# Feed-forward: first mark of a block by a scan and 32x32 transposes on VectorE, its blocks sent to their partitions by DMAs

## The chip, the core and the metric

The kernel runs on one core of a Trainium2 chip: TensorE (PE), VectorE (DVE), ScalarE (ACT), GpSimd (POOL) and SyncE (SP, which here only issues DMAs), with SBUF and PSUM beside them and 16 DMA engines. The metric is the time of one execution in device microseconds; the kernel before takes 1007.56 us (median of 3 runs, 1005.65 to 1009.1).

## What is computed

x is (4, 512, 512): 2048 tokens of width 512. One attention layer (32 heads of 16, 8 key heads) with residual and layer norm, then a sparse feed-forward with residual and layer norm:

```
inter = xf @ c1_w.T @ c2_w.T            # rank 16, 1792 columns
blk   = inter.reshape(tokens, 56, 32)
idx   = argmax(blk, -1) + arange(0, 1792, 32)
h     = relu(sum_m w1[idx] * xf)        # one of 32 rows of w1 in each block
out   = sum_k h * w2t[idx]
x     = layernorm(x + out)
```

`argmax` takes the first of equal maxima, and a token keeps one column of each block of 32.

## The kernel before, in words

The first 593 us (`_attend`) are projections and attention; the change touches only constants there. The feed-forward (`_feed_forward`) works densely: for all 1792 columns it computes h, and sets to zero what was not chosen. It goes over 4 batches b of 512 tokens, and in each over 14 tiles m of 128 columns. One (b, m) is called a slot here, "slot 1,3" is b = 1, m = 3.

In a slot, in TensorE's program order: `inner_up` of this slot (twelve 512-column matmuls into ps_h, three per 128 rows of the contraction, since every operand is split into a high and a low part), `first_marks` (one matmul into ps_z), `inner_down` of the slot before (twelve matmuls into ps_out), and `turn_mask` of the next slot (four bf16 transposes into ps_t). Up to two preparing steps (`slot_steps`) stand between the halves of inner_up and of inner_down.

Preparing steps: a mark step multiplies u (rank 16) by 448 columns of c2 (a chunk; four chunks c to a batch, four token tiles t to a chunk); VectorE reduces each block of 32 to its maximum and compares, which leaves a mask of ones at the maxima, tokens on partitions. In the pick, columns must be on partitions: TensorE turns the mask, ScalarE copies it, and the matmul with `first` (1 on the diagonal, -2 for earlier columns of the same block) gives exactly 1 at the first one. `pick` on VectorE keeps relu(h) where ps_z is 1; ScalarE and GpSimd split the result into g_h and g_l, which ps_out of the next slot reads. Other steps turn tiles of x (xf_sb, xt_h, xt_l), form u ("U"), and in slots 0,4 to 0,7 multiply by wo for the last batch's attention output.

Marks of chunks 1 to 3 of a batch are made in its slots 0-1, 2-5 and 6-7 (6-8 in batch 0), those of chunk 0 in the last slots of the batch before. For b > 0 VectorE also adds ps_out to the residual in slot 0 (`add`), takes statistics in slot 1 and normalises in slot 2.

SP's queue is one program in order. At the start of this half: denominators, w2 tiles 0 and 1, four attention loads, the reciprocals (`inverted`, L936), their spread copy (L938), then by slot the w2 loads (L908), x loads (L902), y loads and stores. A wait on SP holds everything behind it. ScalarE takes w2 tile m+1 before relu of slot m in batch 0 (`high_w2`).

## Time and profile before

| | |
|---|---|
| median of 3 runs | 1007.56 us |
| profiled execution | 998.58 us, span 996.8 us |
| granted TensorE clock, mean | 0.944 |
| busy: PE, DVE, ACT, POOL | 91%, 56%, 44%, 19% |
| L1222 ps_z matmuls in the last 337 us | 49, 390 ns each |
| L1199 ps_t transposes there | 192, 222 ns each |
| L1090 pick there | 49, 691 ns each |

The profile is one execution seen by the hardware profiler. Busy time counts an engine's instructions; matmuls overlap in the pipeline, so their spans add up to more than the time between their starts. "Idle before" is the time in which the engine had nothing running, with what released it. An engine's busy share alone says little: what counts is which wait ends last.

### The profile page before, as it was taken

To read this page: it belongs to the slowest core of one execution; us is meant where nothing else is said; L and a number is where in the kernel's file an instruction comes from. 1 tells how busy PE (TensorE), PEld (TensorE's weight loads), DVE (VectorE), ACT (ScalarE), POOL (GpSimd) and SP (SyncE) were. 2 spreads that over 40 slices of the span, in tenths; PEclk is the share of its full clock that TensorE was granted. 3 is DMA by queue.
4 is the path that set the end of the run, shared out by engine and by line. 5 is a ranking of instruction groups with operands and counts; after the bars stand their busy time and mean duration, and the time that the engine had idled before them with its cause. 6 is when DMAs were issued, how large, how long until landed. Compare 5 with 4: busy or idle time off the path is not lost. (4 is left out here: it accounts for less than half of the span.)

```text
span 996.8 us, 12134 instructions
## 1 busy us (share of the span) xinstructions
PE 908.2 (91%) x4472; PEld 533.0 (53%) x4472; DVE 562.4 (56%) x743; ACT 442.9 (44%) x821; POOL 193.1 (19%) x183
## 2 busy tenths in 40 slices
PE   5868999999899998999989975999999999999995
PEld 3745543333334333343333434777777777777774
DVE  4636567888656885468866533545563365326413
ACT  3302466777654775456765542322222222222231
POOL 6302003730210002100021002333321222122221
PEclk8889999999989998599988978999999999999998
DMA  8466535643342243323433124214030002001101
GB/s 249 160 205 240 169 110 159 175 123 91 91 117 69 76 134 80 97 85 79 135 82 109 34 97 102 82 44 155 14 116 11 1 3 103 2 1 43 42 1 42
DMA packets 50858, 92.99 MB, mean 93 GB/s; under 512 B 5648, under 2 KB 13840, under 8 KB 50288
## 3 DMA queue, kind: packets, MB, share of 16 engines
q1 hardware_dynamic: 49312, 87.05, 29.3%
q0 software_dynamic: 1488, 5.16, 1.9%
q8 instruction: 36, 0.59, 0.2%
q14 instruction: 22, 0.18, 0.1%
HBM read 56.80 MB, written 34.87 MB: 92 GB/s over the span
## 5 line engine op out<-in xcount | busy, mean ns | idle before, releaser
L509 DVE TENSOR_REDUCE neg_max<-ps_max 128x2 f32<-128x1024 f32 x256 | 302.9, 1217 | 90.1 <-PE ps_max L670 89.7
L486 ACT ACTIVATE probs<-ps_st 128x512 f32<-128x512 f32 x496 | 270.2, 595 | 142.6 <-PE ps_st L707 139.7
L707 PE MATMUL ps_st<-q,k 50*128 50x512 f32 x496 | 181.9, 511 | 28.5 <-ACT probs L486 27.6
L707 PEld LDWEIGHTS ps_st<-q,k 50*128 50x128 f32 x496 | 71.9, 192 | 203.1 <-ACT probs L486 156.8
L670 PE MATMUL ps_max<-k,q 48*128 48x512 f32 x512 | 152.8, 452 | 14.0 <-DVE neg_max L509 9.2
L721 PE MATMUL ps_pv<-probs,v 128*32 128x512 f32 x1024 | 147.3, 649 | 5.9 <-ACT probs L486 2.3
L978 POOL TENSOR_TENSOR g_l<-picked,g_h 128x512 fp32r<-128x512 f32 x56 | 73.1, 1306 | 286.9 <-ACT g_h L1017 286.9
L1003 ACT ACTIVATE mask_t<-ps_t 128x512 bf16<-128x512 bf16 x56 | 33.4, 597 | 163.6 <-PE ps_t L1199 163.6
L1211 PE MATMUL ps_h<-xt_h,w_h 128*128 128x512 f32 x224 | 93.8, 419 | 8.0 <-ACT relu L1010 8.0
L1073 DVE TENSOR_REDUCE top<-ps_prep 128x14 f32<-128x448 f32 x62 | 38.6, 623 | 99.0 <-PE ps_prep L1188 98.8
L670 PEld LDWEIGHTS ps_max<-k,q 48*128 48x128 f32 x512 | 75.6, 199 | 28.9 <-DVE neg_max L509 13.5
L1090 DVE SCALAR_TENSOR_TENSOR picked<-ps_z,relu 128x512 f32<-128x512 f32 x56 | 38.7, 691 | 90.6 <-ACT relu L1010 90.6
L1211 PE MATMUL ps_h<-xt_h,w_l 128*128 128x512 f32 x224 | 88.8, 397 | 0.0
L1211 PE MATMUL ps_h<-xt_l,w_h 128*128 128x512 f32 x224 | 88.8, 397 | 0.0
L1010 ACT ACTIVATE relu<-ps_h 128x512 f32<-128x512 f32 x56 | 33.6, 599 | 102.2 <-PE ps_h L1211 102.2
L1234 PE MATMUL ps_out<-w_h,g_h 128*128 128x512 f32 x160 | 71.2, 445 | 0.0
L1234 PE MATMUL ps_out<-w_h,g_l 128*128 128x512 f32 x160 | 63.2, 395 | 0.0
L1234 PE MATMUL ps_out<-w_l,g_h 128*128 128x512 f32 x160 | 63.0, 394 | 0.0
L1211 PEld LDWEIGHTS ps_h<-xt_h,w_h 128*128 128x128 f32 x224 | 43.1, 192 | 15.5 <-ACT relu L1010 8.1
L412 POOL TENSOR_TENSOR att<-att,inv 128x512 f32<-128x512 f32 x12 | 14.8, 1270 | 172.4 <-DMA inv<-reciprocals 172.4
L1211 PEld LDWEIGHTS ps_h<-xt_h,w_l 128*128 128x128 f32 x224 | 42.7, 191 | 9.4
L1211 PEld LDWEIGHTS ps_h<-xt_l,w_h 128*128 128x128 f32 x224 | 43.2, 193 | 6.2
(159 smaller groups left out, 1141.2 us busy)
## 6 DMA issues: line engine op xcount, KB each, us to landing
q_stacks<-parts SPq DMA_DIRECT2D x48, 256.0 KB
q<-q_stacks SPq DMA_DIRECT2D x64, 192.0 KB, 3.6
sums<-stage SPq DMA_DIRECT2D x32, 256.0 KB, 3.4
k<-k_stacks SPq DMA_DIRECT2D x64, 96.0 KB, 3.1
x_raw<-xT SPq DMA_DIRECT2D x16, 256.0 KB, 8.5
yf<-after_attention SPq DMA_DIRECT2D x4, 1024.0 KB, 5.3
w_raw<-w POOLq DMA_DIRECT2D x16, 224.0 KB, 3.1
w_raw<-w SPq DMA_DIRECT2D x14, 256.0 KB, 2.9
```

Source lines behind the costliest of these rows:

```text
L486: nc.scalar.activation(probs[kt % 2][:, r], score_bank(n, r), ACT.Exp, scale=float(HD) ** -0.5).then_inc(exp_done, 1)
L509: nc.vector.tensor_reduce(neg_max[n % 2][:, i // 2, :, i % 2], ps_max[i % 2][:], AX.X, ALU.max, negate=True).then_inc(max_red, 1)
L670: mm = nc.tensor.matmul(ps_max[i % 2][:, a], q[n % QR][64 * a:64 * a + STACK, j, t * P:(t + 1) * P], k_[n % QR][64 * a:64 * a + STACK, :], ...
L707: nc.tensor.matmul(score_bank(n, r), k_[n % QR][64 * a:64 * a + ROWS, kt * P:(kt + 1) * P], q[n % QR][64 * a:64 * a + ROWS, j, :], start=T ...
L721: last = nc.tensor.matmul(ps_pv[32 * r:32 * r + VW], v[f % 2][:, kt, g], probs[kt % 2][:, r], start=(kt == 0), stop=(kt == TT - 1))
L978: nc.gpsimd.tensor_tensor(g_l[m % 2][:], picked[m % 2][:], g_h[m % 2][:].bitcast(F32), ALU.subtract).then_inc(g_ready, 1)
L1003: nc.scalar.activation(mask_t[m % 2][:], ps_t[:], ACT.Copy).then_inc(mask_t_ready, 1)
L1010: nc.scalar.activation(act_r[m % 2][:], ps_h[:], ACT.Relu).then_inc(relu_ready, 1)
L1073: nc.vector.tensor_reduce(top[t % 2][:], src, AX.X, ALU.max).then_inc(prep_half, 1)
L1090: nc.vector.scalar_tensor_tensor(picked[m % 2][:], ps_z[:], 1.0, act_r[m % 2][:], ALU.is_equal, ALU.mult).then_inc(picked_ready, 1)
L1211: last = nc.tensor.matmul(ps_h[:], w[:, k, m * P:(m + 1) * P], xx[b % 2][:, k], start=(k == 0 and n == 0), stop=(k == KT - 1 and n == 2))
L1234: last = nc.tensor.matmul(ps_out[t][:], g[m % 2][:, t * P:(t + 1) * P], w2_tile(*w, m), start=(m == 0 and n == 0), stop=(m == MT - 1 and n ...
```

## The change

The mask turn, its copy and the first-mark matmul go. After the comparison VectorE runs a scan over the 448 columns, rank = rank * doubling + equal, where `doubling` is 2 everywhere and 0 at the start of each block: from the first mark on the value is 1 and is then doubled, so exactly the first marked column has the value 1. VectorE then transposes each 32x32 square, and SP sends the squares to their partitions: 16 DMAs a chunk, each 32 partitions by 3 or 4 blocks by 128 bf16 values. For that u is written with its tokens in another order. The pick compares rank_t in SBUF instead of ps_z. ps_h and ps_prep get two banks each. Relu writes where the pick writes. The w2 tiles are loaded to where their low part will be; the waits for the memory under them move from ScalarE to SP.

```diff
+            def spread_ranks(b, c):
+                i = b * NC + c
+                first, last = c * CH // BLK, (c + 1) * CH // BLK
+                sp.wait_ge(rank_turned, TT * (i + 1))
+                if b:
+                    sp.wait_ge(picked_ready, (b - 1) * MT + (last - 1) // 4 + 1)
+                for o in range(4):
+                    blocks = [n for n in range(first, last) if n % 4 == o]
+                    m = slice(blocks[0] // 4, blocks[-1] // 4 + 1)
+                    for g in range(4):
+                        src = turned[i % 2][BLK * g:BLK * (g + 1), blocks[0] - first:blocks[-1] - first + 1:4]
+                        sp.dma_start(rank_t[BLK * o:BLK * (o + 1), m, P * g:P * (g + 1)],
+                                     src.rearrange("p n t k -> p n (t k)")).then_inc(rank_in[i % 2], DMA)
...
+            spread_ranks(0, 0)
 
             at = (NB - 1) * NH * S
             sp.wait_ge(inverted, 1)
...
+                    if m in (1, 5, 7 if b else 8):
+                        spread_ranks(b, (1, 5, 7 if b else 8).index(m) + 1)
+                    if b + 1 < NB and m == (12 if b else 13):
+                        spread_ranks(b + 1, 0)
...
-                act.wait_ge(mask_turned, i + 1)
-                nc.scalar.activation(mask_t[m % 2][:], ps_t[:], ACT.Copy).then_inc(mask_t_ready, 1)
...
-                nc.scalar.activation(act_r[m % 2][:], ps_h[:], ACT.Relu).then_inc(relu_ready, 1)
+                    act.wait_ge(g_ready, i - 1)
+                nc.scalar.activation(picked[m % 2][:], ps_h[i % 2][:], ACT.Relu).then_inc(relu_ready, 1)
...
-                nc.vector.tensor_copy(u[:], bank[0:80]).then_inc(prep_half, 1)
+                nc.vector.tensor_copy(_by_group(u[:]), _in_order(bank[0:80])).then_inc(prep_half, 1)
...
+                    dve.wait_ge(prep_done, n + 1)
+                    nc.vector.tensor_tensor_scan(rank[:], doubling[:], equal[:], 0.0, ALU.mult, ALU.add
+                                                 ).then_inc(rank_done, 1)
+                    dve.wait_ge(rank_done, TT * i + t + 1)
+                    if i >= 2 and t == 0:
+                        dve.wait_ge(rank_in[i % 2], 16 * DMA * (i // 2))
+                    nc.vector.transpose(turned[i % 2][:, :, t], rank[:].rearrange("p (n k) -> p n k", k=BLK)
+                                        ).then_inc(rank_turned, 1)
...
-                dve.wait_ge(z_done, i + 1)
+                dve.wait_ge(rank_in[c % 2], 16 * DMA * (c // 2 + 1))
                 dve.wait_ge(relu_ready, i + 1)
-                nc.vector.scalar_tensor_tensor(picked[m % 2][:], ps_z[:], 1.0, act_r[m % 2][:], ALU.is_equal,
+                nc.vector.scalar_tensor_tensor(picked[m % 2][:], rank_t[:, m], 1.0, picked[m % 2][:], ALU.is_equal,
                                                ALU.mult).then_inc(picked_ready, 1)
...
-                    last = nc.tensor.transpose(ps_t[:, t * P:(t + 1) * P], mask[:, t, m * P:(m + 1) * P], ident16[:])
-                nc.tensor.matmul(ps_z[:], first[:], mask_t[m % 2][:], start=True, stop=True).then_inc(z_done, 1)
```

SP's order at the start of the feed-forward, before (den_last are the denominators, w_h<-sums the attention loads into memory of w2's high part, w_l<-reciprocals the spread copy, w_raw<-w a w2 tile):

```order
L926 DMA den_last<-sums 128x1x128
L908 DMA w_raw<-w 128x512 x2
L931 DMA w_h<-sums 128x1x512 x4
L936 DMA reciprocals<-inv_den_last 128x128 [waits invertedf]
L938 DMA w_l<-reciprocals 128x1x2048 [waits rdenf_out]
L908 DMA w_raw<-w 128x512 [waits w2_low] x3
L918 DMA yf<-x 128x4x512 [waits attf_split]
```

and now:

```order
L951 DMA w_h<-sums 128x1x512 x4
L918 DMA rank_t<-turned 32x4x128 [waits rank_turned]
L918 DMA rank_t<-turned 32x4x128 x7
L918 DMA rank_t<-turned 32x3x128 x8
L957 DMA reciprocals<-inv_den_last 128x128 [waits invertedf]
L959 DMA w_l<-reciprocals 128x1x2048 [waits rdenf_out]
L928 DMA w_raw<-w 128x512 [waits w2_low] x2
L918 DMA rank_t<-turned 32x3x128 [waits rank_turned]
L918 DMA rank_t<-turned 32x3x128 x7
L918 DMA rank_t<-turned 32x4x128 x8
L928 DMA w_raw<-w 128x512 [waits w2_low]
L938 DMA yf<-x 128x4x512 [waits attf_split]
```

Chunk 0's sixteen DMAs stand between the attention loads and the reciprocals, chunk 1's between w2 tiles 3 and 4.

SP's order in slots 0,8 to 0,10 now (xf_sb are the x loads; chunk 3's DMAs stand ahead of the third of them):

```order
L903 DMA xf_sb<-after_attention 128x512
L928 DMA w_late<-w 128x512 [waits prep_mm,w2_low]
L918 DMA rank_t<-turned 32x3x128 [waits rank_turned]
L918 DMA rank_t<-turned 32x3x128 x7
L918 DMA rank_t<-turned 32x4x128 x8
L903 DMA xf_sb<-after_attention 128x512 [waits prep_mm]
L928 DMA w_late<-w 128x512 [waits w2_low]
L903 DMA xf_sb<-after_attention 128x512 [waits prep_mm]
```

Before, the same x load had only a w2 load ahead of it.

VectorE's order in slot 1,0 before (a mark step, the pick, a mark step, the four adds):

```order
L1073 TENSOR_REDUCE top<-ps_prep 128x14 [waits prep_mm]
L1078 TENSOR_TENSOR mask<-ps_prep,top 128x448 [waits mask_turned,prep_half]
L1090 SCALAR_TENSOR_TENSOR picked<-ps_z,relu 128x512 [waits g_ready,relu_ready,z_done]
L1073 TENSOR_REDUCE top<-ps_prep 128x14 [waits prep_mm]
L1078 TENSOR_TENSOR mask<-ps_prep,top 128x448 [waits prep_half]
L1097 TENSOR_TENSOR yf<-ps_out,yf 128x512 [waits out_mm,yf_in]
L1097 TENSOR_TENSOR yf<-ps_out,yf 128x512 x3
```

and now:

```order
L1093 TENSOR_REDUCE top<-ps_prep 128x14 [waits prep_mm]
L1095 TENSOR_TENSOR equal<-ps_prep,top 128x448 [waits prep_half]
L1103 SCALAR_TENSOR_TENSOR rank<-doubling,equal 128x448 [waits prep_done]
L1108 STREAM_TRANSPOSE turned<-rank 128x14x32 [waits rank_in1,rank_done]
L1116 SCALAR_TENSOR_TENSOR picked<-rank_t,picked 128x512 [waits relu_ready,rank_in0]
L1093 TENSOR_REDUCE top<-ps_prep 128x14 [waits prep_mm]
L1095 TENSOR_TENSOR equal<-ps_prep,top 128x448 [waits prep_half]
L1103 SCALAR_TENSOR_TENSOR rank<-doubling,equal 128x448 [waits prep_done]
L1108 STREAM_TRANSPOSE turned<-rank 128x14x32 [waits rank_done]
L1123 TENSOR_TENSOR yf<-ps_out,yf 128x512 [waits out_mm,yf_in]
L1123 TENSOR_TENSOR yf<-ps_out,yf 128x512 x3
```

Each mark step is four instructions long instead of two, and the pick can wait for the DMAs of its chunk (rank_in).

## Rows read from the trace of the kernel before

**Rows 1.** Windows: us, then busy time of PE, PEld, DVE, ACT, POOL, PEclk, DMA, GB/s

```profile
896.00:912.00 16.00, 16.00 (x77) 12.39 (x76) 12.39 (x25) 4.60 (x9) 4.63 (x4) 1.00 0.00 1
614.00:615.00 1.00, 0.00 (x0) 0.00 (x0) 0.00 (x0) 0.00 (x0) 0.00 (x0) 0.78 0.29 57
```

**Rows 2.** Chain that ended last: start us, us, engine, tile, line

```profile
716.65 1.44 PE ps_h L1211 x6
...
723.12 1.44 PE ps_h L1211 x6
...
946.64 2.80 PE ps_h L1211 x12
949.67 2.79 PE ps_out L1234 x12
952.70 2.80 PE ps_h L1211 x12
```

**Rows 3.** Timeline of VectorE, start of the feed-forward: start us, us, instruction

```profile
593.71 0.62 DVE L1073 TENSOR_REDUCE top<-ps_prep 128x14 f32<-128x448 f32 x1 [10.15 <-PE ps_prep L1188]
594.37 0.62 DVE L1078 TENSOR_TENSOR mask<-ps_prep,top 128x448 bf16<-128x448 f32 x1
594.91 0.61 DVE L1073 TENSOR_REDUCE top<-ps_z 128x14 f32<-128x448 f32 x1
...
596.10 0.94 DVE L1122 RECIPROCAL inv_den_last<-den_last 128x128 f32<-128x128 f32 x1
```

**Rows 4.** Timeline of SP's issues, start of the feed-forward

```profile
597.24 0.48 SPq L936 DMA_DIRECT2D reciprocals<-inv_den_last  x1
603.32 0.59 SPq L938 DMA_DIRECT2D w_l<-reciprocals  x1
603.95 17.89 SPq L908 DMA_DIRECT2D w_raw<-w  x3
633.22 0.38 SPq L918 DMA_DIRECT2D yf<-x  x1
```

**Rows 5.** Timeline of ScalarE and TensorE, slots 0,1 to 0,5

```profile
616.33 0.63 ACT L1025 ACTIVATE w_h<-w_raw 128x512 fp32r<-128x512 f32 x1 [12.69 <-DMA w_raw<-w]
622.40 0.58 PE L1234 MATMUL ps_out<-w_h,g_h 128*128 128x512 f32 x1
639.39 0.63 ACT L1025 ACTIVATE w_h<-w_raw 128x512 fp32r<-128x512 f32 x1 [6.19 <-DMA w_raw<-w]
643.92 0.58 PE L1234 MATMUL ps_out<-w_h,g_h 128*128 128x512 f32 x1
```

**Rows 6.** Timeline of SP's issues in the attention half

```profile
406.21 1.28 SPq L233 DMA_DIRECT2D q<-shift  x2
...
418.59 0.42 SPq L218 DMA_DIRECT2D k<-k_stacks  x1
```

**Rows 7.** DMA issues of the page: transfer, count, KB each, us to landing

```profile
xf_sb<-after_attention SPq DMA_DIRECT2D x12, 256.0 KB, 2.9
...
v_halves<-v_new SPq DMA_DIRECT2D x8, 256.0 KB, 3.6
...
reciprocals<-inv_den SPq DMA_DIRECT2D x3, 64.0 KB, 1.6
```

**Rows 8.** Timeline of VectorE, slots 1,0 to 1,2

```profile
716.52 2.48 DVE L1097 TENSOR_TENSOR yf<-ps_out,yf 128x512 f32<-128x512 f32 x4 [0.19 <-PE ps_out L1234]
...
722.72 2.46 DVE L1102 BATCH_NORM_STATS2 statsf<-yf 128x6 f32<-128x512 f32 x4
...
729.56 1.91 DVE L1115 TENSOR_SCALAR yf<-yf,mvf,rstdf 128x512 f32<-128x512 f32 x4
```

**Rows 9.** Groups of 660 to 997 us: busy, mean ns, idle before

```profile
L978 POOL TENSOR_TENSOR g_l<-picked,g_h 128x512 fp32r<-128x512 f32 x50 | 65.4, 1308 | 250.9 <-ACT g_h L1017 250.9
...
L1017 ACT ACTIVATE g_h<-picked 128x512 fp32r<-128x512 f32 x50 | 31.2, 623 | 0.8 <-DVE picked L1090 0.8
L1010 ACT ACTIVATE relu<-ps_h 128x512 f32<-128x512 f32 x49 | 29.4, 601 | 96.3 <-PE ps_h L1211 96.3
```

More of the change, by code:

```diff
@@ L826, in _feed_forward @@
         den, inv_den = sb("den_last", [P, P]), sb("inv_den_last", [P, P])
-        w2_raw = [sb(f"w2_raw{j}", [P, D]) for j in range(2)]
         x_sb = [sb(f"xf_sb{j}", [P, D]) for j in range(2)]
         top = [sb(f"top{j}", [P, CH // BLK]) for j in range(2)]
-        mask = sb("mask", [P, TT, INTER], BF16)
-        mask_t = [sb(f"mask_t{j}", [P, S], BF16) for j in range(2)]
-        act_r = [sb(f"relu{j}", [P, S]) for j in range(2)]
+        equal, rank = sb("equal", [P, CH], BF16), sb("rank", [P, CH], BF16)
+        doubling = sb("doubling", [P, CH], BF16)
+        turned = [sb(f"turned{j}", [P, CH // BLK, TT, BLK], BF16) for j in range(2)]
+        rank_t = sb("rank_t", [P, MT, S], BF16)
         picked = [sb(f"picked{j}", [P, S]) for j in range(2)]
@@ L1043, in _, with step @@
         def _(dve):
-            def step(kind, b, s, bank):
+            def step(kind, b, s):
                 n = number(b, s, kind)
-                half = halves(n)
+                half, bank = halves(n), ps_prep[n % 2]
                 dve.wait_ge(prep_mm, n + 1)
@@ L1118, in _ @@
             for t in range(TT):
-                step("prep", 0, marks(0, t), (ps_prep, ps_z)[t % 2])
+                step("prep", 0, marks(0, t))
                 if t == 1:
@@ L1126, in _ @@
                     if steps:
-                        step(*steps[0], ps_prep)
+                        step(*steps[0])
                     pick(b, m)
                     if len(steps) > 1:
-                        step(*steps[1], ps_prep)
+                        step(*steps[1])
                     if b and m == 0:
@@ L1161, in _, with step @@
         def _(pe):
-            def step(kind, b, s, bank, banks=1):
+            def step(kind, b, s):
                 n = number(b, s, kind)
-                if n >= banks:
-                    pe.wait_ge(prep_done, n - banks + 1)
+                bank = ps_prep[n % 2]
+                if n >= 2:
+                    pe.wait_ge(prep_done, n - 1)
                 if kind == "wo":
@@ L1253, in _ @@
                     if steps:
-                        step(*steps[0], ps_prep)
+                        step(*steps[0])
                     if b * MT + m:
                         inner_up(b, m, (2, 3))
-                    first_marks(b, m)
                     if b * MT + m:
@@ L1260, in _ @@
                     if len(steps) > 1:
[L1261 removed]
+                        step(*steps[1])
                     if b * MT + m:
                         inner_down(*before, (2, 3))
[L1264 to L1265 removed]
             inner_down(NB - 1, MT - 1, (0, 1, 2, 3))
```

122 lines of the change are left out of this document (50 added, 72 removed).

## Prediction

> **What bounds the kernel now.** I read the windows first, then the chain, then the timeline where the chain breaks. In the feed-forward half TensorE never pauses: in 896 to 912 us it is busy 16.00 of 16 while VectorE is busy 12.39, in one of the stretches where a new batch starts [rows 1]. The chain shows the same as back-to-back groups: twelve ps_h matmuls, twelve ps_out, and between the groups gaps of 0.23 (first-mark matmul) and 0.24 us (mask turn) [rows 2]. A slot (one m of one batch b) lasts 6.06 us without a preparing step and 6.47 us with two [rows 2]. So what leaves TensorE shortens the end, as long as VectorE, the DMA queue and the loads keep up. The exception is the start of the half: SP sends the reciprocals at 597.24, their spread copy at 603.32 and w2 tile 2 right behind it [rows 4]; ScalarE gets that tile only at 616.33, 12.69 us idle, and the next ps_out group starts at 622.40 [rows 5].
>
> **What is removed.** Per slot 0.23 + 0.24 = 0.47 us of TensorE; 56 slots make 26.3 us, the most that the change can give. ScalarE loses one 0.6 us copy a slot and the pool engine some constants; both wait for others, so nothing. The second ps_h bank and the second ps_prep bank free no time where TensorE is never idle. POOL's two constant fills lie ahead of their first reader: nothing.
>
> **What is added on VectorE.** Each of the 64 mark steps gets a scan and a transpose. The old step: the comparison starts 0.66 after the reduce, the next reduce 0.54 later (1.20) [rows 3]. The new one waits for each result: 0.66 + 0.66 + scan + transpose. No row shows either operation. Low bound of each: one pass over the elements, 0.54; high: two passes, 1.24 (twice the 0.62 of a 448-element operation [rows 3]). The scan makes each element wait for the product and sum before it, a reason to leave the low end: I take 0.95 for it, and one pass, 0.62, for the transpose, less the overlap of 0.08 with what follows. Step: 0.66 + 0.66 + 0.99 + 0.54 = 2.85 us (2.4 to 3.8).
> The Trainium skill ("DVE: opcode table, instruction layouts, handler registers and perf-mode slots", Datapath and trigger behaviour) states that the built-in tensor_tensor_scan runs at half throughput; no row here shows it. By that rule the scan would be near the upper bound of mine and the sum some 3 to 6 us longer.
>
> **What is added on the DMA queue.** Each of the 16 chunks of 448 columns is sent by 16 DMAs from SP. An issue of equal shapes on both sides takes 0.42 us, of unequal ones 1.28/2 = 0.64 [rows 6]; with the 0.04 gap I take 0.47: 7.5 us a chunk (6.1 at the 0.38 of the shortest issue shown [rows 4], 10.2 at 0.64). A small transfer lands in 1.6 us [rows 7]; with the wait ahead I take 2.0. So from a chunk's last transpose to its pick there are 9.5 us, during which everything behind it on SP stands still. Before, the same path was a turn, a copy and a matmul within a slot.
>
> **The sum, stage by stage.** After a pick, g is ready 0.62 + 1.31, about 2.0 us later [rows 9]; relu ends 0.7 after its ps_h group [rows 9]; ps_out of a slot starts 3.0 us into the next slot's TensorE work.
> (a) *Start.* VectorE starts at 593.71: four steps and the reciprocal (0.94 [rows 3]) end at 593.7 + 11.4 + 0.9 = 606.0. Chunk 0's spread stands in the program ahead of the reciprocals, so SP sends until 613.6, the reciprocals go then (before: 597.24), and after a 2 us landing the spread copy at 616.1. From there to the w2 tile behind it before took 13.0 us (603.32 to 616.33 [rows 4, 5]), bytes that are the same now: 629.1. Then relu, pick and g: ps_out of slot 0,1 starts at 632.9 instead of 622.40. The pick of slot 1 stands ahead of chunk 1's last mark step on VectorE: that step ends at 633.8, SP sends to 641.4, and only then w2 tile 4, which relu of slot 3 stands behind: it ends at 645.2, g is ready at 647.9. The attention split follows the same pick (4 x 0.62: 648.4), the y load follows it, and w2 tile 5, which came 6.2 us after the y load was issued (633.22 to 639.39 [rows 4, 5]), comes at 654.6: relu, pick and g of slot 4 end at 658.3. Before, that ps_out group started at 643.92 [rows 5]: +14.4, with what the slots up to there save already in it.
> (b) *The remaining slots* save 50.5 x 0.47 = -23.7.
> (c) *Slot 0,10.* The x load for the third turned tile now stands behind chunk 3's spread. Counted from slot 8: its last mark step ends at 8.3, SP is free at 15.8, the load lands 2.9 later [rows 7] at 18.7; TensorE wants it at 13.9. +4.8.
> (d) *Start of batch 1.* Its chunk 0 is finished in slot 13: at 5.2 us from that slot's start, landed at 14.7. The pick of slot 1,0 could run at 9.7. VectorE then has, in program order, pick, step, four adds (2.48), step, pick, step, statistics (2.46 and some 0.4 of small ones), step, pick, split (two of about 0.7) and norm (1.91), step, pick [rows 8]. That puts g of slots 0 to 3 at 17.2 (adds done from 18.8 to 20.9), 26.3, 35.5, 42.3; TensorE, starting each slot when the one before ends, would want them at 15.0, 24.8, 32.3 and 41.7. Slot 0 waits for the first add: +3.8 + 1.5 + 3.2 + 0.6 = +9.1.
> (e) *Starts of batches 2 and 3.* There chunk 0 is finished a slot earlier and lands in time; what is left is VectorE's queue alone: g of slots 1, 2, 3 is late by 1.2, 3.1 and 0.5: +4.8 each, +9.6.
> In all 14.4 - 23.7 + 4.8 + 9.1 + 9.6 = +14.2 us. Pauses of this length need not cost clock: after the long pause before 616 the granted clock fell only in 614 to 615, five us after TensorE had stopped [rows 1]. From slot 4 of a batch on VectorE needs 4.9 us of a 6.2 us slot, 6.3 of 6.0 in slots 6 and 7, and the 2.7 us by which a pick may be late cover that.
> The profiled execution took 998.58 us with a span of 996.8; the median of the runs is 1007.56. I put the difference on the median: 1007.6 + 14.2 = 1021.8, 1022 us.
>
> **Rivals.**
> 1. *The cheap end, no change.* Scan in one pass (step 2.4), issue 0.42, landing 1.6. The same walk gives +10.3 at the start, +3.1 in (c), +4.8 in (d) and twice +2.2 in (e), against 23.7: -1.1, 1006.5 us. For it: the scan's inputs are 448 elements like the comparison's. Against: it needs all three cheap.
> 2. *Faster.* VectorE's queue never reaches TensorE, since a step costs 2.0 or less, and an issue 0.38. Then mostly the start is left: SP frees the reciprocals no earlier than 602.6 + 6.1 = 608.7, 11.5 after before, of which some 7 survive at slot 4, and 2 in (c): 26.3 - 9 - 4 at batch 1 = 13 us gained, 994. Against: the step's two existing halves alone are 1.3, and both new operations would have to be 0.35.
> 3. *Transfers bound by their packets.* A chunk is 1792 packets of 256 bytes. A transfer with 8 packets of 512 bytes an engine lands in 1.6, one with 32 in 3.6 [rows 7]: 0.083 us a packet, 7 packets 0.58 us a DMA, already over the issue of 0.47. If a packet below 512 bytes costs double, a chunk takes 18.6 us instead of 7.5 and its pick comes 11 us later: twice at the start, once each in (c) and (d), and about 5 at each of the later starts: +54 on top, 1077. For it: the packets are smaller than any in the trace before. Against: the slope is from transfers that touch HBM among others. The Trainium skill ("DMA: Bandwidth & Descriptors", Specifications) says that below 512 B the engine does read-modify-write; the same page (Why small descriptors are slow) exempts transfers within SBUF. The trace shows neither.
> 4. *The change does not do what it says:* mask matmuls stay. The instruction order has none left; no chance given.
>
> **How the numbers follow.** This kernel's measurement tells a change from none at about 0.3%, 3 us. Forecast with its spread (1011 to 1040, steps 2.5 to 3.3, issues 0.42 to 0.64): 0.70. Rival 1: 0.13, within 3 us. Rival 2: 0.11. Rival 3: 0.06. Faster 0.13 (rival 2 and a little of rival 1), same 0.11, slower 0.76. The range, 1004 to 1042: the low end takes in rival 1, the high end an issue at 0.64 (two spreads at the start, one each in (c) and (d), 2.7 each: +11) with a step of 3.2 (+8, since 0.1 us on a step costs 0.4 at the start, 0.1 in (c), 0.6 in (d), twice 0.5 in (e)).
>
> **What would show it.** Reciprocals issued near 613 and w2 tile 2 at ScalarE near 629. Scan mean near 950 ns, transpose near 620, SP issues of rank_t near 420 ns. TensorE pauses in slot 0,10 on the x load, in slots 1,1 to 1,4 on g, and two or three in batches 2 and 3, none elsewhere; slots of 5.6 to 6.0 us between them. Wrong would be: a pick that waits for rank_t everywhere (rival 3), or no pause after 700 us (rival 2).

## Result and profile after

The changed kernel takes 1052.43 us (median of 4 runs, 1047.95 to 1057.05), the kernel before on the same chip 1006.61 (4 runs, 999.81 to 1009.1): ratio 1.047, interval 1.040 to 1.054. It is slower, as the forecast had it, but by 45.8 us and not by 14, and outside its range. Some executions of a kernel are slower as a whole, and ratios, here and below, leave them out, while a median counts them: the traced one of e1_start (4192 us, every matmul slow), one each of e3_noscan and v2_after_order, and two of before in the experiments.

The profiled execution of after took 1047.95 us with a span of 1046.1. The feed-forward half starts at 601.53 us and lasts 444.6 us; before, it started at 592.93 and lasted 403.9. So of the 49.3 us between the two spans 40.7 lie in the changed half. The other 8.6 lie in the attention half, in which the change touches only constants, the place of some tiles and the order in which u is written. In the ten traces of this study that share after's attention half it ends anywhere from 592.1 to 609.9 us, and in the three traces with before's from 592.9 to 602.2, so I do not count the 8.6 for the change. All numbers below are from the changed half, counted from its start where slots of two kernels are compared.

The costliest groups of the page of after that are new or changed (busy, mean ns of one, idle before), and the spread among its transfers:

```profile
L1007 POOL TENSOR_TENSOR g_l<-picked,g_h 128x512 fp32r<-128x512 f32 x56 | 72.5, 1295 | 314.5 <-ACT g_h L1038 314.5
...
L1103 DVE TENSOR_TENSOR_SCAN rank<-doubling,equal 128x448 bf16<-128x448 bf16 x64 | 81.8, 1278 | 2.2
L1116 DVE SCALAR_TENSOR_TENSOR picked<-rank_t,picked 128x512 f32<-128x512 bf16 x56 | 37.3, 665 | 69.2 <-ACT picked L1031 44.0
L1093 DVE TENSOR_REDUCE top<-ps_prep 128x14 f32<-128x448 f32 x64 | 39.2, 612 | 48.4 <-PE ps_prep L1215 48.4
...
rank_t<-turned SPq DMA_DIRECT2D x128, 32.0 KB, 1.9
```

The scan's mean is 1278 ns where I had taken 950. A DMA of the spread lands in 1.9 us (2.0 taken, with the wait ahead of it). The timeline of SyncE's issues of after, at the start of the half (start us, us, instruction), answers to [rows 4]:

```profile
615.39 10.37 SPq L918 DMA_DIRECT2D rank_t<-turned  x16
625.81 0.59 SPq L957 DMA_DIRECT2D reciprocals<-inv_den_last  x1
627.61 0.65 SPq L959 DMA_DIRECT2D w_l<-reciprocals  x1
...
646.33 10.24 SPq L918 DMA_DIRECT2D rank_t<-turned  x16
656.61 0.59 SPq L928 DMA_DIRECT2D w_raw<-w  x1
666.02 0.39 SPq L938 DMA_DIRECT2D yf<-x  x1
```

Where a spread stands alone in the timeline its sixteen issues take 10.2 to 10.9 us, some 0.64 each. It is not the DMA engines that hold them: they are busy for 21% of 616 to 625 us, and where only four are sent (e2_quarter) the four take 2.67 us, about as much for each. ScalarE and TensorE of after, the same tiles as in [rows 5]:

```profile
640.76 0.63 ACT L1046 ACTIVATE w_h<-w_raw 128x512 fp32r<-128x512 f32 x1 [12.32 <-DMA w_raw<-w]
...
672.32 0.63 ACT L1046 ACTIVATE w_h<-w_raw 128x512 fp32r<-128x512 f32 x1 [10.22 <-DMA w_raw<-w]
```

```profile
644.73 0.80 PE L1243 MATMUL ps_out<-w_h,g_h 128*128 128x512 f32 x1 [7.05 <-POOL g_l L1007]
...
676.28 0.50 PE L1243 MATMUL ps_out<-w_h,g_h 128*128 128x512 f32 x1 [2.17 <-POOL g_l L1007]
```

What TensorE waited for in the changed half of after (us in total, times, longest):

```profile
PE ps_out L1243 <- POOL g_l L1007: 36.8, 11, 9.9
PE ps_out L1243 <- DVE yf L1123: 11.7, 3, 7.7
PE ps_prep L1203 <- DMA xf_sb<-after_attention: 8.6, 1, 8.6
PE ps_prep L1215 <- DVE equal L1095: 6.8, 5, 2.5
```

The waits are where the prediction put them (the start, the x tile of slot 0,10, the starts of the later batches), and they are longer. And they are not all: busy time of PE, PEld, DVE, ACT and POOL in the changed half, with TensorE's granted clock after them, in after and then in before:

```profile
601.50:1046.10 444.60, 369.02 (x1540) 295.65 (x1540) 303.08 (x436) 78.27 (x130) 100.64 (x78) 0.92 0.22 61
```

```profile
592.90:996.80 403.90, 382.79 (x1820) 294.19 (x1820) 180.76 (x308) 105.55 (x186) 95.75 (x76) 0.98 0.15 49
```

Idle time of TensorE rose from 21.1 to 75.6 us. Its busy time fell by 13.8 us only, though 280 instructions with 26.3 us are gone: the clock fell from 0.98 to 0.92. Stretches of 4 us of after show where:

```profile
664.00:668.00 4.00, 4.00 (x11) 2.95 (x11) 3.93 (x5) 0.00 (x0) 1.44 (x1) 0.57 0.21 47
716.00:720.00 4.00, 0.00 (x0) 0.00 (x0) 0.00 (x0) 0.00 (x0) 0.00 (x0) 0.50 0.37 72
720.00:724.00 4.00, 3.02 (x9) 2.57 (x10) 1.38 (x2) 0.63 (x1) 0.00 (x0) 0.50 0.99 336
764.00:768.00 4.00, 2.27 (x5) 1.83 (x6) 3.93 (x8) 0.00 (x0) 0.00 (x0) 0.50 0.00 0
```

A clock of 0.50 is the lower level, 1.2 GHz. The matmuls behind the pause of 8.6 us, from 720.98 us on, take 0.63 us and more, those from 725.68 on 0.39 again; those from 644.73 on, behind the pause of 7.05, take 0.63 too. Not every pause costs: behind the one of 2.17 us before 676.28 the clock is 1.00 (676.3 to 680), behind the one of 2.53 before 783.06 it is 0.66 (783 to 788).

### The profile page after: what moved, and what is told of

It reads as the page before. It is cut to its first block and busy times, and to the rows that moved or that the text cites. A ratio compares the mean times of both kernels' runs of the same rounds, so it can differ in the third digit from the quotient of the medians.

```text
span 1046.1 us, 11746 instructions
## 1 busy us (share of the span) xinstructions
PE 900.6 (86%) x4192; PEld 537.1 (51%) x4192; DVE 682.9 (65%) x871; ACT 415.6 (40%) x765; POOL 196.7 (19%) x179
## 5 line engine op out<-in xcount | busy, mean ns | idle before, releaser
L1038 ACT ACTIVATE g_h<-picked 128x512 fp32r<-128x512 f32 x56 | 35.4, 632 | 173.0 <-DVE picked L1116 170.6
L1228 PE MATMUL ps_h<-xt_h,w_h 128*128 128x512 f32 x224 | 89.8, 401 | 0.0
L1228 PE MATMUL ps_h<-xt_l,w_h 128*128 128x512 f32 x224 | 89.2, 398 | 0.0
L1031 ACT ACTIVATE picked<-ps_h 128x512 f32<-128x512 f32 x56 | 33.3, 594 | 130.4 <-PE ps_h L1228 130.4
L1103 DVE TENSOR_TENSOR_SCAN rank<-doubling,equal 128x448 bf16<-128x448 bf16 x64 | 81.8, 1278 | 2.2
L1116 DVE SCALAR_TENSOR_TENSOR picked<-rank_t,picked 128x512 f32<-128x512 bf16 x56 | 37.3, 665 | 69.2 <-ACT picked L1031 44.0
L1243 PE MATMUL ps_out<-w_l,g_h 128*128 128x512 f32 x160 | 66.7, 417 | 0.0
L1243 PE MATMUL ps_out<-w_h,g_l 128*128 128x512 f32 x160 | 66.7, 417 | 0.0
L1243 PEld LDWEIGHTS ps_out<-w_h,g_h 128*128 128x128 f32 x160 | 32.9, 206 | 59.3 <-POOL g_l L1007 40.1
```

The lines of the kernel that those rows point to most:

```text
L1103: nc.vector.tensor_tensor_scan(rank[:], doubling[:], equal[:], 0.0, ALU.mult, ALU.add).then_inc(rank_done, 1)
L1116: nc.vector.scalar_tensor_tensor(picked[m % 2][:], rank_t[:, m], 1.0, picked[m % 2][:], ALU.is_equal, ALU.mult).then_inc(picked_ready, 1)
L1228: last = nc.tensor.matmul(ps_h[i % 2][:], w[:, k, m * P:(m + 1) * P], xx[b % 2][:, k], start=(k == 0 and n == 0), stop=(k == KT - 1 and n ...
L1243: last = nc.tensor.matmul(ps_out[t][:], g[m % 2][:, t * P:(t + 1) * P], w2_tile(*w, m), start=(m == 0 and n == 0), stop=(m == MT - 1 and n ...
```

## Experiments

All ratios are to the kernel before on the same chip. "Half" is the length of the feed-forward half in the trace (after: 444.6 us).

**e0_removed.** Before without the mask path of TensorE and ScalarE; every pick compares with a constant.

```diff
-                    first_marks(b, m)
...
-                    if b * MT + m + 1 < NB * MT:
-                        turn_mask(*divmod(b * MT + m + 1, MT))
```

> The kernel before with the mask turn, its copy and the first-mark matmul left out and the pick comparing a constant tile of ones (so every column is kept): only what the change takes from TensorE. Theory A (the removed TensorE work is worth its full 0.47 us in each of 56 slots): 26 us faster than before, feed-forward half 378 us instead of 404. Rival (the gaps are filled by something else that TensorE waits for, so the gain was never there): under 10 us.

Measured: 984.95 us, ratio 0.978 (0.972 to 0.983); half 381.3, 22.6 less than before.

```profile
595.80:977.10 381.30, 356.68 (x1540) 288.01 (x1540) 186.38 (x308) 79.00 (x130) 97.31 (x77) 0.97 0.17 52
```

These are the same 1540 matmuls as in after. So this trace splits after's half: against it after has 51.0 us more idle (75.6 to 24.6) and 12.3 us more busy time (369.02 to 356.68) for the same work. Expected were 26 us, and over 10 of them came, so the rival fell. The removal gives 22.6 of the 26.3 us: busy time falls by 26.1, and 3.5 come back as idle time, 3.3 of it at the start, where TensorE only comes sooner to waits that stay: the stall for w2's tile 2 is 8.5 us instead of 8.0, there is a second wait for relu of 1.7, and the waits for marks are longer. At ps_out of slot 0,4 e0_removed is 2.6 us behind before; from there to the end it gains 25.2. The ps_out matmuls show where part of the 12.3 us lies, e0_removed first and after second (mean ns behind the bar):

```profile
L1230 PE MATMUL ps_out<-w_h,g_h 128*128 128x512 f32 x160 | 64.2, 401 | 0.0
```

```profile
L1243 PE MATMUL ps_out<-w_h,g_h 128*128 128x512 f32 x160 | 69.4, 434 | 47.2 <-POOL g_l L1007 35.4 <-DVE yf L1123 11.7
```

The first form of the ps_h matmuls takes 405 and 401 ns. It is the group behind the pauses that got longer.

**e1_start and e6_start_again.** Chunk 0's spread behind the reciprocals, their spread copy and w2's tile 2.

```diff
-            spread_ranks(0, 0)
...
                         load_w2(m + 2)
+                    if b == 0 and m == 0:
+                        spread_ranks(0, 0)
```

> The changed kernel with chunk 0's sixteen DMAs moved behind the reciprocals, their spread copy and w2 tile 2 on SP; nothing else. Theory A (SP's order costs the start): reciprocals issued some 8 us after the half begins instead of 24, w2 tile 2 early, ps_out of slot 0,1 some 11 us earlier, and 9 to 14 us faster than the changed kernel (near 1040 us). Rival B (VectorE's marks and the landing of the chunks set the start anyway): under 4 us.

> The same kernel as e1_start (after, with chunk 0's spread behind the reciprocals, their 1 MB copy and w2's tile 2), for its trace. Theory (behind the copy and ahead of the spread, tile 2 lands at 615 or before, so that the 12.3 us wait of ScalarE goes, but tile 3 and the tiles behind it now stand behind the spreads of chunks 0 and 1, which follow each other): the offset of slot 0,1 falls by 6 us and more than half of it is lost again by slot 0,9. Rival: the 6 us stay to the end, and x tile 2 still costs 8.6 us at slot 0,10. Time 1040 to 1047 in both; the slots tell them apart.

Measured: e1_start 1046.07 us, ratio 1.035 (1.029 to 1.041), some 12 us less than after by the ratios. Its own trace is not read, and e6_start_again, the same kernel, stands in for it; one run: 1046.27 us, half 440.9 (-3.7). Its reciprocals go 8.1 us after the half's start, and ScalarE no longer waits for w2's tile 2, as expected. But by the picks slot 0,1 is only 5.2 us earlier than after's, slot 0,6 3.8, and the last slot 3.8: the pick of slot 0,0 now stands at 28.0 us where it stood at 25.6, since it waits for the spread, which goes later. So about a quarter of the gain at the start is lost when the next spreads reach the loads; more than half was expected. The 12 us include the attention half's scatter; the 3.7 us of the traces are the safer number for the change's own part, and by them theory A (9 to 14 us) fell and rival B (under 4) holds.

**e2_quarter.** 4 of a chunk's 16 DMAs are sent; the rest of rank_t holds ones, written once by GpSimd at the start of the half.

```diff
-                    for g in range(4):
+                    for g in range(1):
...
             nc.gpsimd.memset(doubling[:], 2.0).then_inc(half_set, 1)
+            nc.gpsimd.memset(rank_t[:], 1.0).then_inc(doubling_set, 1)
```

> The changed kernel with 4 of the 16 DMAs of each chunk (the other rows of rank_t are set to 1 once and not sent, so picks are wrong there): SP is held 2.6 us a chunk instead of 10.2. Theory A (SP held by its issues is the larger part of the loss): about 15 us less at the start, 7 in slot 0,10, 8 at batch 1, little at batches 2 and 3: 25 to 32 us faster than the changed kernel, near 1024 us. Rival C (VectorE's longer steps are the larger part): 8 to 15 us. Where each chunk lands it also shows what the packets cost apart from the issue.

Measured: 1022.54 us, ratio 1.014 (1.009 to 1.019); half 420.0 (-24.6): idle 56.4 (-19.2), busy 363.63 (-5.4). That is just short of theory A (25 to 32 us) and far above rival C (8 to 15). A DMA lands in 1.9 us here too. The experiment has a cost of its own at the start, where 15 us had been expected and slot 0,4 came only 5.9 us sooner: the fill of rank_t takes GpSimd 6.08 us and stands ahead of the constants of the scan, and VectorE's first scan waits 4.65 us for it:

```profile
597.23 6.08 POOL L995 MEMSET rank_t<- 128x7168 bf16 x1
...
603.51 2.02 DVE L1106 TENSOR_TENSOR_SCAN rank<-doubling,equal 128x448 bf16<-128x448 bf16 x1 [4.65 <-POOL doubling L997]
```

So a quarter of the spread alone would be worth some 29 us (an estimate: 24.6 and the 4.65 of that wait, which the start's chain passes on).

**e3_noscan.** The comparison's result is transposed directly; every mark in a block counts as its first.

```diff
-                    nc.vector.tensor_tensor_scan(rank[:], doubling[:], equal[:], 0.0, ALU.mult, ALU.add
-                                                 ).then_inc(rank_done, 1)
-                    dve.wait_ge(rank_done, TT * i + t + 1)
```

> The changed kernel with the scan left out; the comparison's result is transposed and sent (of equal maxima all are kept). A mark step falls from about 3.2 to 1.9 us. Theory A: 5 us at the start, 1 in slot 0,10, 7 at batch 1 and 6 each at batches 2 and 3, 20 to 25 us faster than the changed kernel, near 1030 us; the starts of batches 2 and 3 no longer pause. Rival D (SP's issues alone hold everything, VectorE has time): under 8 us and the pauses stay.

Measured: 1015.92 us, ratio 1.006 (1.003 to 1.010); half 413.6 (-31.0): idle 51.0 (-24.6), busy 362.57 (-6.5). That is more than theory A's 20 to 25, and rival D (under 8) fell. With 81.8 us of scans gone the half is 31.0 shorter, and at the start of batch 2 TensorE's pauses for ps_out are 0.72 and 1.15 us, at that of batch 3 0.54 and 1.92.

**e5_quarter_noscan.** Both edits together.

> After with a quarter of the spread (4 of 16 DMAs a chunk, the other squares hold ones) and without the scan. Each alone took 24.6 and 31.0 us off the feed-forward half's 444.6 us. Theory (the costs stand one behind the other at the starts of batches and at slot 0,10, each adding its own time): both together take 50 to 56 us, the half lasts 389 to 395, the time is 995 to 1000. Rival (both end the same pauses and the clock's losses go with the pauses, so either alone already gives back a good part of what both give): together 35 to 45 us, the half lasts 400 to 410, the time is 1005 to 1015, and a start stall of about 8 us stays as in the kernel without mask work at all.

Measured: 990.39 us, ratio 0.979 (0.974 to 0.985); half 384.0, 60.6 less than after:

```profile
592.10:976.10 384.00, 354.55 (x1540) 288.97 (x1540) 226.32 (x372) 78.75 (x130) 102.88 (x79) 0.95 0.18 56
```

More than the sum of the two (55.6), and 2.7 us above e0_removed. So both costs stand one behind the other on the same paths. It too has the fill of rank_t, for which VectorE waits 4.66 us: at ps_out of slot 0,4 it is 6.2 us behind e0_removed, and from there to the end 3.5 us faster, for a reason that no run here separates (the second banks of ps_h and ps_prep are one difference). So the rest of the change, the transposes and the four DMAs, costs nothing that shows. The rival (35 to 45 us) fell, and the theory's order holds, but 60.6 us lie beyond its range of 50 to 56: it is the clock that came back as well, TensorE's busy time being 14.5 us less than in after.

**e4_nopool.** GpSimd computes 32 of g_l's 512 columns, the others stay zero.

```diff
-                nc.gpsimd.tensor_tensor(g_l[m % 2][:], picked[m % 2][:], g_h[m % 2][:].bitcast(F32),
+                nc.gpsimd.tensor_tensor(g_l[m % 2][:, 0:32], picked[m % 2][:, 0:32], g_h[m % 2][:, 0:32].bitcast(F32),
```

> After with GpSimd's subtraction of g_l done on 32 of its 512 columns (the others are zero, set once at the start; GpSimd's halves of w2 stay whole). In the trace of after the scan took 1.09 us where GpSimd stood still and 1.72 to 1.75 us beside a subtraction of GpSimd, and GpSimd's own 1.26 became 1.6 to 2.1. Theory (the two engines slow each other): the scans' mean falls from 1278 to about 1100 ns (only those beside w2's halves stay long), and each slot's chain to g_l is 1.2 us shorter, which is on the path only where PE waits for g_l (11 waits in after): the time falls by 12 to 20 us, to 1032 to 1040. Rival (the scan is as long as it is for a cause of its own, such as the order of its operands): the mean stays near 1278 and the gain is that of the chain alone, 8 to 13 us.

Measured: 1036.96 us, ratio 1.029 (1.025 to 1.034); half 431.3 (-13.3). Over the whole half the scans' mean fell from 1278 to 1164 ns (about 1100 expected). The scans from 770 us to the end, where no half of w2 is made any more, in after and then in e4_nopool:

```profile
L1103 DVE TENSOR_TENSOR_SCAN rank<-doubling,equal 128x448 bf16<-128x448 bf16 x41 | 51.9, 1266 | 1.4
```

```profile
L1105 DVE TENSOR_TENSOR_SCAN rank<-doubling,equal 128x448 bf16<-128x448 bf16 x41 | 44.7, 1091 | 1.4
```

1091 ns with GpSimd nearly still (its subtraction of 32 columns takes 0.25 us), 1266 with its full work: the theory holds, and the rival's 1278 fell. How the 13.3 us divide between the shorter scans and the chain to g_l, which the edit shortens as well, this run doesn't tell. In after the timelines of VectorE and of GpSimd show single cases:

```profile
603.63 1.09 DVE L1103 TENSOR_TENSOR_SCAN rank<-doubling,equal 128x448 bf16<-128x448 bf16 x1
...
628.99 1.72 DVE L1103 TENSOR_TENSOR_SCAN rank<-doubling,equal 128x448 bf16<-128x448 bf16 x1
...
649.77 4.68 DVE L1167 TENSOR_TENSOR yf<-w_h,w_l 128x512 f32<-128x512 f32 x4
...
661.35 4.64 DVE L1171 TENSOR_TENSOR xt_l<-yf,xt_h 128x512 fp32r<-128x512 f32 x4
```

```profile
628.51 1.26 POOL L1007 TENSOR_TENSOR g_l<-picked,g_h 128x512 fp32r<-128x512 f32 x1 [21.53 <-ACT g_h L1038]
629.73 2.06 POOL L999 TENSOR_TENSOR w_l<-w_raw,w_h 128x512 fp32r<-128x512 f32 x1
...
650.59 1.61 POOL L1007 TENSOR_TENSOR g_l<-picked,g_h 128x512 fp32r<-128x512 f32 x1 [3.90 <-ACT g_h L1038]
652.17 1.74 POOL L999 TENSOR_TENSOR w_l<-w_raw,w_h 128x512 fp32r<-128x512 f32 x1
```

The scan that starts at 628.99 ends at 630.71, 0.94 us after GpSimd's first subtraction has ended at 629.77; GpSimd's second one, begun at 629.73, ends at 631.79, 1.08 after the scan's end. Each seems to wait for the other's instruction and then runs at about its own length. The four multiplications at 649.77, both of whose operands are in SBUF, take 4.68 us; the same ones of before took 2.48, with no work of GpSimd beside them. The Trainium skill ("SBUF — State Buffer", section "SBUF: two separate sides") says that VectorE and GpSimd share a pair of ports as a lock that one instruction holds for its whole length, and names VectorE's operations with two SBUF inputs, against a GpSimd operation that reads SBUF; the trace agrees within 0.2 us.

**v1_before_w2.** Before, with w2's tiles 2 and 3 ahead of the reciprocals' spread copy.

```diff
             sp.wait_ge(rden_out, DMA)
+            load_w2(2)
+            load_w2(3)
             sp.dma_start(inv.rearrange("p r t -> p (r t)"),
...
-                    if b == 0 and m + 2 < MT:
+                    if b == 0 and 1 < m < MT - 2:
```

> The kernel before, with w2's tiles 2 and 3 issued ahead of the 1 MB copy that spreads the reciprocals. Before, ScalarE waited 12.69 us for tile 2 at 616.33 and PE 7.96 us at 617.50, and the copy was ahead of tile 2 on the queue. Theory: tile 2 lands at 606 to 607, the stall of 7.96 goes, and the copy, 5 us later, is not missed, as its first reader stands in slot 0,2: 6 to 9 us faster, ratio 0.991 to 0.994. Rival (the wait moves to the copy: it lands at 620 or later, the attention scaling at slot 0,2 is late, and with it the projection of slot 0,4 and w2's tile 8 and later): no change, ratio 0.998 to 1.002.

Measured: 1003.29 us (12 runs), ratio 0.9965 (0.9938 to 0.9992); half 399.6 (-4.3). The 7.96 us stall is gone, and VectorE waits at slot 0,2 as the rival said:

```profile
628.71 2.50 DVE L1143 TENSOR_TENSOR yf<-w_h,w_l 128x512 f32<-128x512 f32 x4 [5.47 <-DMA w_l<-reciprocals]
```

Half theory, half rival: the ratio lies between the two ranges (0.991 to 0.994, 0.998 to 1.002). Of the kernels here that leave nothing out it is the only one faster than before, by about 0.35%, with 1 just outside the interval.

**v2_after_order.** After with w2's tiles 2 and 3 and the spread copy ahead of chunk 0's spread (four semaphores for w2), and batch 1's x tiles 2 and 3 issued from ScalarE.

```diff
-            spread_ranks(0, 0)
...
+            load_w2(2)
+            load_w2(3)
...
+                    if b == 0 and m == 0:
+                        spread_ranks(0, 0)
...
+                    if b == 0 and m in (9, 10):
+                        i = TT + m - 7
+                        act.wait_ge(prep_mm, number(1, m - 9) + 1)
+                        nc.scalar.dma_start(x_sb[i % 2][:], x1[i * P * D:(i + 1) * P * D].rearrange("(p d) -> p d", p=P)
+                                            ).then_inc(x_in[i % 2], DMA)
```

> After with its order of DMAs mended and nothing else: w2's tiles 2 and 3 and then the reciprocals' 1 MB copy ahead of chunk 0's spread (four semaphores for w2 in place of two, so that tile m waits for tile m-4), and x tiles 2 and 3 of batch 1 issued by ScalarE's queue in slots 0,9 and 0,10, so that they don't stand behind chunk 3's spread. Theory (10 us of issues stood ahead of other loads at the start and at slot 0,10): the 8.6 us wait for x goes, the start's waits shrink by 10 to 14, and the starts of batches 1 to 3 stay as they are: the time falls by 18 to 24 us against after, to 1028 to 1034, ratio to before 1.02 to 1.027. Rival (the spread's own length binds, wherever it stands, because the marks of chunk 0 are what slot 0,0 waits for): only the x wait goes, 8 to 10 us, about 1043.

Measured: 1041.86 us, ratio 1.031 (1.026 to 1.036), but a half of 443.9, only 0.7 us shorter than after's. So the lower time comes from the attention half (it ended at 593.08 in this trace), and the theory, 18 to 24 us, fell for the changed half, and so did the rival, by which the x wait would go: TensorE waits 11.2 us for x in place of 8.6. Slot 0,4 came 6.2 us earlier than in after, and it was lost again. ScalarE's timeline, then SyncE's, then TensorE's say why:

```profile
707.88 0.63 ACT L1049 ACTIVATE wo_h<-w_late 128x512 fp32r<-128x512 f32 x1 [10.21 <-DMA w_late<-w]
...
709.83 0.33 ACTq L1061 DMA_DIRECT2D xf_sb<-after_attention  x1
```

```profile
694.64 10.27 SPq L918 DMA_DIRECT2D rank_t<-turned  x16
704.96 1.06 SPq L928 DMA_DIRECT2D w_late<-w  x2
```

```profile
713.86 1.09 PE L1211 MATMUL ps_prep<-ident,xf_sb 128*128 128x128 f32 x4 [10.48 <-DMA xf_sb<-after_attention]
```

The x load was off the spread's queue, but ScalarE, which issues it, stood itself behind a w2 tile on that queue.

**v3_pool_queue.** After with w2's tiles 2 to 13 and x tiles 2 and 3 of batch 1 issued by GpSimd, with semaphores of their own.

```diff
             low_w2(0)
+            late_w2(2)
...
                         low_w2(m + 1)
+                    if b == 0 and m + 3 < MT:
+                        late_w2(m + 3)
+                    if b == 0 and m in (9, 10):
+                        late_x(m - 7)
```

> After with w2's tiles 2 to 13 and batch 1's x tiles 2 and 3 issued by GpSimd, each where its buffer comes free, so that on SyncE's queue only the spreads, two x tiles, y and the stores are left. Mending the order on SyncE's queue (v2_after_order) had left the feed-forward half at 443.9 us, with 10 us waits for w_late at 707.88 and for xf_sb at 713.86, both behind a spread. Theory (it is the in-order queue: every load that stands behind a chunk's 16 issues is 10 us late): ScalarE's waits of 12.3, 4.4, 10.2 and 10.8 us for w2 and PE's of 8.6 us for x go, the half falls by 14 to 20 us to 425 to 431, and the starts of batches 1 to 3 stay as they are (7.7 us waits for the spread itself). Time 1033 to 1040. Rival (the loads are only second: the spread itself is as late, and PE waits as long for the picks): the half falls by less than 8 us.

Measured: 1048.71 us, ratio 1.039 (1.030 to 1.049); half 439.5 (-5.1). Slot 0,4 stands 14.9 us earlier than in after and slot 0,10 15.5, which is the theory's size; but x now waits in GpSimd's order (12.0 us in two waits), and slot 0,11 keeps 6.8. The rival's number (under 8) came out, not for its reason.

**v4_soon.** v3_pool_queue with chunk 0's marks of batches 2 and 3 a slot sooner, and their spread issued in slot 11.

```diff
-            late = {8: (U,), 9: (marks(0, 0),), 10: (marks(0, 1),), 11: (marks(0, 2),), 12: (marks(0, 3),)}
+            late = {8: (U, marks(0, 0)), 9: (marks(0, 1),), 10: (marks(0, 2),), 11: (marks(0, 3),)}
```

> v3_pool_queue with chunk 0's marks of batches 2 and 3 taken one slot sooner (slot 8 takes u and the first of them, slots 9 to 11 the others) and their spread issued from slot 11 in place of 12. In after, slots 2,0 to 2,2 and 3,0 to 3,2 each took 9 to 10 us instead of 6.0, and so much that slot 2,3 stood 7.4 us behind slot 1,13's offset. Theory (the spread of 10.2 us plus landing of 1.9 us does not fit between the last mark and the next batch's first pick, and one slot of 5.7 us sooner it does): the two starts lose at least 3 of those 7.4 us each: 5 to 10 us faster than v3. Rival (the start is lengthened by DVE's own work there, adds, statistics and marks with the scan, not by the spread): within 2 us of v3.

Measured: 1041.95 us, ratio 1.034 (1.025 to 1.043); half 437.5, 2.0 less than v3, where the theory had 5 to 10. From slot 1,13 to slot 2,3 it takes 33.5 us where after took 35.3, and 32.7 in place of 33.9 a batch later. The rival holds: these two starts are set mostly by VectorE's own work, not by the spread.

**v5_act_x.** v4_soon with the two x tiles issued by ScalarE, as in v2.

> v4_soon with batch 1's x tiles 2 and 3 issued by ScalarE's queue in slots 0,9 and 0,10 in place of GpSimd's, where they had come late (PE waited 13.2 us for them, twice, once behind w2's halves in GpSimd's own order). With w2 off SyncE's queue, ScalarE no longer stands behind a spread there. Theory (with all loads off the spreads' queue what is left in slots 0,10 and 0,11 is the spread of chunk 3 itself, 10.2 us of issues and 1.9 of landing behind the last mark): the 13.2 us of waits shrink to 2 to 6, of which the pick of slot 0,10 takes a part back: 5 to 9 us faster than v4, the feed-forward half 428 to 433, 1033 to 1037, ratio to before 1.022 to 1.030; it stays slower than before, since DVE's longer steps and the spread of each chunk stay. Rival (the waits change their name only): within 3 us of v4.

Measured: 1032.34 us, ratio 1.026 (1.020 to 1.031); half 429.4, 15.2 less than after and 8.1 less than v4, as expected (5 to 9 us, half 428 to 433). TensorE's waits for x fell from 13.2 to 7.7 us, not to 2 to 6; the two largest groups left are those of after:

```profile
PE ps_out L1267 <- POOL g_l L1020: 28.5, 11, 10.2
PE ps_out L1267 <- DVE yf L1144: 9.5, 3, 7.8
PE ps_prep L1227 <- DMA xf_sb<-after_attention: 7.7, 2, 6.8
```

So of the 40.7 us in the changed half, the order of the queues accounts for some 13, and with v4's earlier marks for 15. The rest needs shorter mark steps or fewer issues, as e5_quarter_noscan shows.

## Why the prediction was wrong

The direction, the places and the order of events were right; the sizes were not, and one term was missing. Stage by stage, net change against before, measured as the time between the picks of two slots in the two traces:

| stretch | predicted | measured |
|---|---|---|
| start to slot 0,4 | +14.4 | +24.3 |
| slots 0,4 to 0,9 | -2.4 | -2.0 |
| slots 0,9 to 0,13 | +2.9 | +10.5 |
| to slot 1,13 | +2.5 | +5.5 |
| to slot 2,13 | -1.8 | +2.1 |
| to slot 3,13 | -1.8 | +0.8 |
| to the end | 0 | -0.5 |

(The predicted column takes the prediction's terms (a) to (e), with 0.47 us off for each slot beyond 0,4; that is 51 slots, where the sum took 50.5.) A pick can be late and not hold TensorE. By TensorE's own ps_out groups, of slots 0,4, 0,8, 0,12, 1,12, 2,12 and 3,12, the measured column is +23.8, -2.4, +8.6, +8.2, +2.1, +0.8 and -0.4: some 2 us of the third row belong to the fourth.

Against e0_removed, which has the same matmuls, the same stretches of after show what was added, and as what (idle and busy time of TensorE in us, clock; e0_removed first, after second):

| to ps_out of slot | idle | busy | clock | added | term |
|---|---|---|---|---|---|
| 0,4 | 13.4, 29.7 | 40.2, 45.1 | 0.82, 0.76 | 21.2 | (a) |
| 0,8 | 0.0, 0.0 | 31.6, 31.3 | 1.00, 1.00 | -0.2 | |
| 0,12 | 0.0, 8.6 | 27.2, 29.2 | 1.00, 0.86 | 10.6 | (c) 4.8 |
| 1,12 | 0.0, 11.8 | 85.7, 89.2 | 1.00, 0.95 | 15.3 | (d) 9.1 |
| 2,12 | 0.0, 7.8 | 85.7, 87.1 | 1.00, 0.98 | 9.2 | (e) 4.8 |
| 3,12 | 0.0, 6.8 | 80.4, 81.3 | 1.00, 0.98 | 7.7 | (e) 4.8 |
| the end | 11.2, 10.9 | 6.0, 5.9 | 0.79, 0.81 | -0.4 | |

**What is removed: 26.3 predicted, 22.6 measured** (e0_removed), and not where the sum failed. TensorE's busy time did fall by 26.1; what is missing was lost at the start, where TensorE only comes sooner to the same stall. The sum had counted only the slots beyond 0,4, with 23.7 us, and there e0_removed gains 25.2.

**The issue: 0.47 taken, 0.64 measured.** This is the step on the DMA queue that failed. [Rows 6] had both values, 0.42 for equal and 0.64 for unequal shapes on the two sides; the spread is of the second kind, since it goes from a range of turned with a step in it to a block of another form, and I took a value near the first. At the start it is directly visible: the reciprocals went 24.3 us after the half's start (predicted 20.7), of which 2.9 are issues; w2's tile 2 came 13.1 us after the copy, as predicted (13.0); ps_out of slot 0,1 was 3.2 us late; at ps_out of slot 0,4 the delay against the prediction had grown to 9.4. To the 3.2 the second spread added 2.7, the scan of 1.72 us in the mark step ahead of it 0.6, and the four subtractions of the attention split, which release the y load with w2's tile 5 behind it, 2.1 (4.64 us instead of 2.5, with GpSimd beside them): 8.6 of the 9.4. The multiplications of 4.68 us cost nothing here: VectorE waited 3.28 us for relu of slot 0,3 afterwards. In slot 0,10 SyncE was free 19.4 us after slot 0,8 began (15.8 predicted), 2.7 of it issues, and TensorE waited 8.6 us for x instead of 4.8.

**The mark step: 2.85 taken, some 3.0 measured with GpSimd still.** With the scan at 1.09 us the step at 602.32 lasts 3.01 (to 605.33), the one at 609.36 2.95; at 628.99 the scan takes 1.72, and the steps beside GpSimd are 0.6 us longer. Some 0.14 us of this is the scan itself, which the range had; that VectorE and GpSimd hold each other up was in no term. The prediction's own sensitivities give for a mean scan of 1278 ns, a step of 3.2, 8 us (7.4 if they are added up). In each part of (e) the sum was 4.8 us for VectorE's queue, while the steps there, two a slot, made slots 2,0 and 2,1 9.6 and 10.0 us long by the picks, and 9.2 and 7.7 us were added.

**"Pauses of this length need not cost clock": wrong.** This is the term that the sum put at nothing. I read it from one window around the start of before, where the clock fell five microseconds after TensorE had stopped [rows 1]. But that row is inside a pause and says only when the clock falls, not what the work behind it costs. The trace of before had the answer in the matmuls behind the same pause, which take 0.63 us and more in place of 0.39:

```profile
617.50 0.79 PE L1211 MATMUL ps_h<-xt_h,w_h 128*128 128x512 f32 x1 [7.96 <-ACT relu L1010]
618.09 0.63 PE L1211 MATMUL ps_h<-xt_l,w_h 128*128 128x512 f32 x1
```

After has a dozen pauses over 2 us in this half, and TensorE works at 1.2 GHz behind those of 4.1 us and more, at once or within a microsecond; shorter ones went either way. The price is 12.3 us of busy time against e0_removed for the same matmuls. That the loss hangs on the pauses is borne out by the stretches: in the one without a pause the busy time is not longer than in e0_removed and the clock is 1.00, in each one with pauses it is longer. The other kernels with the same matmuls agree in the main: idle time of 75.6, 67.5, 56.4, 51.0 and 29.4 us (after, e4_nopool, e2_quarter, e3_noscan, e5_quarter_noscan) goes with a busy time of 369.0, 363.8, 363.6, 362.6 and 354.6 (e0_removed, with 24.6 and 356.7, is at the same low end). But the sum of the idle time doesn't fix the loss: v2_after_order and v3_pool_queue, with 72.9 and 69.0 us, are busy for 371.0 and 370.5, more than after. No kernel varied the pauses alone, so the size per pause stays open.

Together, from before to after: at ps_out of slot 0,4 there are 23.8 us where (a) had 14.4, 9.4 more. Beyond it 42.2 us were added to e0_removed where (c), (d) and (e) had 23.5, 18.6 more, and 25.2 were taken away where the sum had 23.7, 1.5 more. That makes the 26.5 us between the predicted 14.2 and the measured 40.7. Against e0_removed as a whole after has 63.3 us more, 51.0 of idle time and 12.3 of clock. The prediction had worked out 11 us for the issue at 0.64 and 8 for the step at 3.2, which is where the range's end of 1042 stood. Both of these high ends came true at once, and the clock came on top; the three together would be more than the 26.5, so these rates overlap or are somewhat high. How the 51.0 us of idle time divide between issue and scan can't be told exactly, as each shortens the same waits: 24.6 and 31.0 alone, 60.6 together, with clock. What is left open is also the difference of the medians, 45.8 us, against the traces' 40.7: the attention half's scatter is larger than that.

**The rivals.** Rival 1 (cheap end) and 2 (faster) fell on the scan and the issue. Rival 3 (packets; its sum is 1076, not 1077) fell: the issues fill SyncE's time, a DMA lands in 1.9 us, and the DMA engines are busy for 21% of such a stretch, so a chunk is not bound by its 256-byte packets. Rival 4 was not the case: 1540 matmuls and transposes are left of 1820. The rule of the Trainium skill ("DVE: opcode table, instruction layouts, handler registers and perf-mode slots", Datapath and trigger behaviour) that I had set beside the scan, half throughput, would have given 3 to 6 us more; the scan with GpSimd still, 1.09 us, lies halfway between my 0.95 and the 1.24 that it stood for, so it bears the rule's direction out.

## What to carry to other kernels

When a step is moved to an engine that is three quarters busy where batches start (12.39 of 16 us here), its price is set in the few places where the second engine's work comes in a row (starts of batches), so work these out with the duration that holds there, beside what GpSimd does at the time. Small DMAs cost their issue first: count issues by the row of the nearest shape, and ask of each in-order queue what stands behind them, also what stands behind a wait for something behind them. And a pause of TensorE can cost more than its length: add the time at the lower clock behind it, at the rate that a kernel with the same matmuls and fewer pauses shows.

## What was not expected of the hardware

- A tensor_tensor_scan over 448 bf16 elements takes 1.09 us alone, against 0.62 for a comparison of 448, and up to 1.75 beside a subtraction of GpSimd, whose 1.26 us becomes 2.06 (after). Four multiplications of 512 elements from SBUF take 2.48 us alone and 4.68 beside GpSimd.
- The issue of a DMA from 32 partitions of one tile to 32 of another, with a stride on one side, takes 0.64 us on SyncE, and about as much when only 4 are sent in a row instead of 16 (0.67), and it lands 1.9 us after it was issued.
- Behind pauses of 4.1 to 9.9 us TensorE works at 1.2 GHz; of the shorter ones, 2.17 us left the clock at 1.00 and 2.53 us was followed by 0.66 (after).
- In ten traces with the same instructions in it the attention half lasted 592.1 to 609.9 us, with the granted clock between 0.94 and 0.89: a scatter of nearly half of the change's effect. A difference between two kernels here is better read from the half that changed than from the whole time.
